# Attention scores and maxima as pairs of 64-row products, in eight long stretches a unit

## The reference, cut to what matters

```
x = layernorm(x)                                       # per token, 256 channels
q, k, v = x @ w_q[h], x @ w_k[h], x @ w_v[h]           # 16 heads of 64
a = softmax(where(query < key, -inf, q @ k.T / 8))     # 1024 x 1024 per head
y = a @ v ;  out = concat_heads(y) @ w_o
```

## Time and profile before

| | |
|---|---|
| median of three runs | 2221.36 us (2218.73 to 2223.20) |
| span of the profiled execution | 2217.0 us |
| PE, PEld, DVE busy | 97%, 72%, 66% of the span |
| ACT, POOL busy | 45%, 62% |
| one regular unit of the attention | 32.39 us |

### The profile page before, as it was taken

One profiled execution on the slowest core, in us unless ns is written; L12 is line 12 of the kernel. 1 busy time (PEld: TensorE's weight loads), 2 busy tenths in 40 slices (PEclk: granted clock), 3 DMA queues, 4 the chain that ended last, 5 costly groups with the idle time before them and its releaser, 6 DMA issues.

```text
span 2217.0 us, 34079 instructions
## 1 busy us (share of the span) xinstructions
PE 2144.5 (97%) x12130; PEld 1600.3 (72%) x12130; DVE 1463.6 (66%) x3344; ACT 1003.0 (45%) x1908; POOL 1375.0 (62%) x1242
## 2 busy tenths in 40 slices
PE   7998999999999999999999999999999999999998
PEld 5446888889876666766667666567666588889997
DVE  7375687676757666476775577874877636975654
ACT  6202543454355554254553354552554425444443
POOL 4313675777457676456674567664677846777774
PEclk9999999999999999999999999999999899999999
DMA  4524553655432212221322131221220244545552
GB/s 133 185 95 122 136 141 97 150 141 134 96 96 58 58 49 57 67 77 49 77 62 70 52 86 48 58 67 58 67 77 24 74 134 115 135 114 146 122 150 40
DMA packets 145048, 206.04 MB, mean 93 GB/s; under 512 B 19432, under 2 KB 112112, under 8 KB 144880
## 3 DMA queue, kind: packets, MB, share of 16 engines
q1 hardware_dynamic: 120304, 170.30, 25.7%
q0 software_dynamic: 24576, 33.57, 9.1%
HBM read 130.03 MB, written 39.85 MB: 77 GB/s over the span
## 4 chain that ended last, share of the span: by engine, by line
PE 74%; DVE 8%; POOL 4%; issue 3%; ACT 2%; DMA 1%; SPq 1%; POOLq 0%; DVEq 0%; ACTq 0%
PE psum L1337 12%; PE psum L1506 11%; PE psum L1358 11%; PE psum L1408 8%; PE psum L1471 7%; PE psum L1487 6%; PE psum L1531 5%; PE psum L1422 4%; PE psum L1436 3%; PE psum L1516 3%; POOL t_acc L2478 2%; DVE f_hhi L2215 2%; DVE f_hlo L2217 1%; PE psum L1449 1%; DVE f_wlo L2190 1%
## 5 line engine op out<-in xcount | busy, mean ns | idle before, releaser
L1782 ACT ACTIVATE t_p<-psum 128x512 f32<-128x512 f32 (+3 forms) x768 | 323.6, 492 | 294.0 <-PE psum L1487 285.7
L2478 POOL TENSOR_TENSOR t_acc<-t_acc,t_p 128x1024 f32<-128x1024 f32 (+3 forms) x256 | 416.9, 1629 | 14.5 <-ACT t_p L1782 0.5
L2397 POOL TENSOR_TENSOR f_wlo<-f_wst,f_whi 128x256 fp32r<-128x256 f32 x256 | 221.8, 943 | 149.0 <-ACT f_whi L1715 148.9
L1506 PE MATMUL psum<-t_p,t_v 128*64 128x512 f32 (+3 forms) x1536 | 289.2, 497 | 5.0 <-POOL t_p L2458 5.0
L1358 PE MATMUL psum<-f_whi,f_hhi 128*128 128x256 f32 x992 | 286.4, 289 | 7.1 <-DVE f_hlo L2217 7.0
L1358 PE MATMUL psum<-f_whi,f_hlo 128*128 128x256 f32 x992 | 280.8, 283 | 0.0
L1358 PE MATMUL psum<-f_wlo,f_hhi 128*128 128x256 f32 x992 | 280.6, 283 | 0.0
L2215 DVE CAST f_hhi<-f_h 128x512 fp32r<-128x512 f32 x256 | 142.2, 556 | 203.5 <-ACT f_h L1733 202.9
L1733 ACT ACTIVATE f_h<-psum 128x512 f32<-128x512 f32 x256 | 153.0, 598 | 271.5 <-PE psum L1337 260.0
L1471 PE MATMUL psum<-t_qa,t_ka 128*128 128x512 f32 (+3 forms) x768 | 224.1, 372 | 1.8 <-DVE t_mx L2263 0.8
L2478 POOL TENSOR_TENSOR t_acc<-t_p 128x768 f32<-128x768 f32 x64 | 134.5, 2102 | 136.9 <-PE psum L1516 133.6
(11 more groups left out here) (297 smaller groups left out, 4452.4 us busy)
## 6 DMA issues: line engine op xcount, KB each, us to landing
f_wst<-in_L_ffn_w SPq DMA_DIRECT2D x64, 1024.0 KB, 5.3
t_ka<-t_ka SPq DMA_DIRECT2D x64, 256.0 KB, 3.5
t_qb<-t_qa SPq DMA_DIRECT2D x64, 256.0 KB, 3.9
t_wk<-wkT SPq DMA_DIRECT2D x32, 256.0 KB, 4.3
t_wq<-wqT SPq DMA_DIRECT2D x32, 256.0 KB, 4.0
t_wv<-wvT SPq DMA_DIRECT2D x16, 512.0 KB, 4.7
normal<-f_xy SPq DMA_DIRECT2D x5, 1024.0 KB, 5.6
a_x<-in_L_attn_a_x SPq DMA_DIRECT2D x4, 1024.0 KB, 8.1
```

What stands on the lines that cost most here:

```text
L1506: m = pe.matmul(k.bank[6][i * DH:(i + 1) * DH, q0:BANK], v[:, kt, vs:vs + DH], p[:, i, q0:BANK], start=(kt == 0), stop=(kt == last), skip_ ...
L1782: act.activation(p[:, i, q0:], k.bank[bank][:, q0:], ACT.Exp, scale=1.0 / float(np.sqrt(k.DH))).then_inc(k.drained[bank], 1)
L2397: m = pool.tensor_tensor(t["wlo"][n % 2][:, i, ks], t["wst"][:, i, ks], t["whi"][n % 2][:, i, ks].bitcast(F32), ALU.subtract)
L2478: pool.tensor_tensor(acc[:, :, q0:], (p0 if kt == 1 else acc)[:, :, q0:], p[:, :, q0:], ALU.add).then_inc(k.p_acc, 1)
```

## The change

The q and k parts are kept as four tiles `khi`, `klo`, `qhi`, `qlo` in which the pair's two heads lie in the two halves of the partitions, as the projection leaves them. Nothing is doubled or moved: `qk_double` and the DMA of `max_rows` are gone. A tile's scores are four products a head, each with 64 rows: high.high, high.low, low.high, and ones against `t_neg`. All are issued as pairs, head 0 in the upper half of the array and head 1 in the lower, into two banks. All maxima parts are such pairs too.

`t_neg` now holds the negated maxima spread over 64-row halves (row n has block n's maxima at block n's columns, zero elsewhere). DVE makes it in one instruction of 72 rows by 1024 columns from the transposed maxima and a tile of minus ones. It is one buffer, and the first scores of a unit wait on PE, ahead of all their products, for it (`wait_drained(("rows", u))`).

A unit is now eight stretches: for g = 0, 1, 2 a row stretch (scores of four key tiles and, after each, the next unit's maximum part) and a column stretch (denominators and weighted values of these tiles); a stretch of full products after the column stretch of g = 0 (`first_work`: projections, values, output) and after that of g = 2 (`last_work`: projection, the transposed maxima, projection, output). There are eight `t_p` buffers.

```diff
-        self.NP = 4
+        self.NP = 8
...
-            kept = [{}, {}]
-            for m in ("ka", "qa", "kb"):
-                for hd in kept:
-                    hd[m] = sb("t_" + m, [P, L], F32R)
-            qb = t["qb"][n] = sb("t_qb", [P, 2, L], F32R)
-            t["heads"][n] = [dict(hd, qb=qb[:, i, :]) for i, hd in enumerate(kept)]
+            t["heads"][n] = {m: sb("t_" + m, [P, L], F32R) for m in ("khi", "klo", "qhi", "qlo")}
...
+        t["minus"], t["mx1"] = sb("t_minus", [P, NBLK]), sb("t_mx1", [P, 2, NBLK - KPC])
...
+        t["neg"] = sb("t_neg", [P, NBLK, P], F32R)
...
-        parts = [(n, c, min(BANK, (n + 1) * P - c * BANK))
-                 for c in range(self.NC) for n in range(self.KPC * c, self.NBLK)]
-        return [p for p in parts if p[2] > BANK // 2], [p for p in parts if p[2] <= BANK // 2]
+        return [[(n, c, (n + 1) * P - c * BANK if diagonal else BANK) for n in range(n0, n0 + self.KPC)]
+                for n0, c, diagonal in ((0, 0, True), (self.KPC, 0, False), (self.KPC, 1, True))]
+
+    def stretch_tiles(self, g):
+
+        return [(min(g, 1), self.KPC * max(g - 1, 0) + i) for i in range(self.KPC)]
 
     def head_rows(self, i):
 
-        return slice(i * self.DH, (i + 1) * self.DH), slice((1 - i) * self.DH, (2 - i) * self.DH)
+        return slice(i * self.DH, (i + 1) * self.DH)
+
+    def qk_place(self, j):
+
+        return (0, 2, 1, 3)[j] + 1
...
+        def project(u, *parts):
+            for j in parts:
                 self.qk_product(u, j)
                 self.qk_low(u, j)
...
+        def normalize(u, c):
+            self.sum_rows(u, c)
+            self.scale_rows(u, c)
+            if u % NHP == NHP - 1:
+                b = u // NHP
+                if b < B - 1:
+                    self.out_load(b, c)
+                extra.append(output(b, c))
+
+        def row_halves(u, g):
+
+            for i, (c, kt) in enumerate(k.stretch_tiles(g)):
                 self.scores(u, c, kt)
...
+                if u + 1 < U:
+                    self.row_max(u + 1, *maxima[g][i])
+                    self.part_max(u + 1, *maxima[g][i])
+                yield
+
+        def column_halves(u, g):
+
+            if g == 0 and u:
+                self.divide(u - 1, 1)
+            for c, kt in k.stretch_tiles(g):
+                self.weigh(u, c, kt)
+                self.add_up(u, c, kt)
+            if g == 1:
+                self.divide(u, 0)
+                normalize(u, 0)
+            elif g == 0 and u:
+                normalize(u - 1, 1)
+
+        def first_work(u):
+
+            yield from project(u + 1, 1, 3)
+            if (u + 2) % NHP == 0 and u + 2 < U:
+                yield from prepare((u + 2) // NHP)
+            for _ in range(value_pieces((u + 1) % NHP)):
+                next(state["values"])
+                yield
+            yield from pieces(2)
+
+        def last_work(u):
+
+            if u + 2 < U:
+                yield from project(u + 2, 0)
+            self.max_rows(u + 1)
+            yield
+            if u + 2 < U:
+                yield from project(u + 2, 2)
+            yield from pieces(3)
...
+            for _ in project(1, 0, 2):
+                pass
+            for u in range(U - 1):
                 if u % NHP == 0:
                     state["rows"] = between(u // NHP)
+                if u + 2 < U:
+                    self.qk_load(u + 2)
+                for g in range(3):
+                    for _ in row_halves(u, g):
+                        pass
+                    column_halves(u, g)
+                    pump(state["rows"])
+                    if g != 1:
+                        for n, _ in enumerate((last_work if g else first_work)(u)):
+                            pump(state["rows"])
+                            if state["scored"] < 2 or n < 2:
+                                pump(state["route"])
+            yield from last_unit(U - 1)
...
+    def row_max(self, u, n, c, w):
+
+        k, pe, heads = self.k, self.e, self.k.t["heads"][u % 2]
+        self.wait_ge(k.a_qk, 2 * k.NC * u + (2 if n < k.KPC else 4))
+        banks = [self.take(("max", u, n, c, i), self.work_bank()) for i in range(2)]
+        for i, bank in enumerate(banks):
+            hd = k.head_rows(i)
+            pe.matmul(k.bank[bank][:, 0:w], heads["qhi"][hd, n * P:(n + 1) * P], heads["khi"][hd, c * BANK:c * BANK + w],
+                      start=True, stop=True).then_inc(k.filled[bank], 1)
...
+        pe.transpose(k.bank[bank][0:k.MROWS, 0:P], t["mx"][:], k.ident[:]).then_inc(k.filled[bank], 1)
...
-    def high_scores(self, u, c, kt):
+    def scores(self, u, c, kt):
 
         k, pe, t = self.k, self.e, self.k.t
         q0, qs, ks = self.score_slices(c, kt)
-        for i in range(2):
-            bank = self.take(("st", u, c, kt, i), self.work_bank())
-            hd = t["heads"][u % 2][i]
-            pe.matmul(k.bank[bank][:, q0:], hd["ka"][:, ks], hd["qa"][:, qs], start=True, stop=False)
-
-    def scores(self, u, c, kt):
-        k, pe, t = self.k, self.e, self.k.t
-        q0, qs, ks = self.score_slices(c, kt)
-        banks = [k.where["st", u, c, kt, i][0] for i in range(2)]
+        heads = t["heads"][u % 2]
         if c == 0 and kt == 0:
-            self.wait_ge(k.t_const_d, 4 if u else 2)
             hp = u % k.NHP
             v = min(4 + 2 * hp, 16) - 1
             self.wait_drained(("v", u // k.NHP, v // 4, v % 4))
-            for h in range(2):
-                self.wait_ge(k.q_dup[u % 2][h][1], DMA * (u // 2 + 1))
-            self.wait_ge(k.q_rows[u % 2], DMA * (u // 2 + 1))
-        for i in range(2):
-            hd = t["heads"][u % 2][i]
-            pe.matmul(k.bank[banks[i]][:, q0:], hd["kb"][0:k.QROWS, ks], hd["qb"][0:k.QROWS, qs], start=False,
-                      stop=True).then_inc(k.filled[banks[i]], 1)
+            for j in range(2 * k.NC):
+                self.wait_drained(("qk", u, j))
+            self.wait_drained(("rows", u))
+        banks = [self.take(("st", u, c, kt, i), self.work_bank()) for i in range(2)]
+        neg = t["neg"][:].rearrange("p n j -> p (n j)")
+        for a, (keys, queries) in enumerate((("khi", "qhi"), ("khi", "qlo"), ("klo", "qhi"))):
+            for i, bank in enumerate(banks):
+                hd = k.head_rows(i)
+                pe.matmul(k.bank[bank][:, q0:], heads[keys][hd, ks], heads[queries][hd, qs], start=(a == 0), stop=False)
+        for i, bank in enumerate(banks):
+            hd = k.head_rows(i)
+            pe.matmul(k.bank[bank][:, q0:], k.ones[hd, :].bitcast(F32R), neg[hd, qs], start=False,
+                      stop=True).then_inc(k.filled[bank], 1)
...
-        for i in range(2):
-            hi, (first, _) = t["heads"][u % 2][i]["qa" if j // k.NC else "ka"], k.head_rows(i)
-            act.copy(hi[first, c * BANK:(c + 1) * BANK],
-                     k.bank[bank][i * k.DH:(i + 1) * k.DH, :]).then_inc(k.a_qk, 1)
+        hi = t["heads"][u % 2]["qhi" if j // k.NC else "khi"]
+        act.copy(hi[:, c * BANK:(c + 1) * BANK], k.bank[bank]).then_inc(k.a_qk, 1)
...
+        dve.memset(t["mx"][:], 0.0).then_inc(k.t_const_d, 1)
+        dve.memset(t["neg"][:].bitcast(F32), 0.0).then_inc(k.t_const_d, 1)
+        dve.scalar_tensor_tensor(out=t["minus"][:], in0=k.ident[:, 0:k.NBLK], scalar=-1.0,
+                                 in1=k.ident[:, k.DH:k.MROWS], op0=ALU.mult, op1=ALU.subtract).then_inc(k.t_const_d, 1)
...
+        self.wait_ge(k.a_qk, 2 * k.NC * u + k.qk_place(j))
+        dve.tensor_tensor(heads["qlo" if is_q else "klo"][:, cs], k.bank[bank],
+                          heads["qhi" if is_q else "khi"][:, cs].bitcast(F32), ALU.subtract).then_inc(k.drained[bank], 1)
...
-        if u > 1:
-            self.wait_ge(k.q_rows[u % 2], DMA * (u // 2))
-        dve.tensor_scalar(t["neg"][u % 2][:], k.bank[bank][0:2 * k.NBLK, 0:P], -1.0, None, ALU.mult).then_inc(k.drained[bank], 1)
+        self.wait_ge(k.t_const_d, 3)
+        if u:
+            self.wait_filled(("st", u - 1, 1, 2 * k.KPC - 1, 1))
+        rows = slice(0, k.MROWS)
+        dve.tensor_tensor(t["neg"][rows], spread(k.bank[bank][rows, 0:P], 1, k.NBLK), spread(t["minus"][rows], 2, P),
+                          ALU.mult).then_inc(k.drained[bank], 1)
...
-    def qk_double(self, u, is_q):
-        k, sp, DH = self.k, self.e, self.k.DH
...
-            src = hd["qa" if is_q else "ka"][first, :]
-            dst = hd["qb"][0:DH, :] if is_q else hd["ka"][other, :]
...
-            sp.dma_start(dst.bitcast(F32), src.bitcast(F32)).then_inc(k.q_dup[u % 2][i][is_q], DMA)
...
-        sp.dma_start(row.bitcast(F32), t["neg"][u % 2][:].bitcast(F32)).then_inc(k.q_rows[u % 2], DMA)```

PE's rows are shown where the kernel before has its mixed order, in a unit with values (`t_p,t_v` is `weigh`, `t_acc,ones` is `divide`, `t_ka,t_qa` with x4 or in the short widths a maximum; order lists a weight pair by its output rows):

```order
L1516 MATMUL psum<-t_acc,ones 64x512 x2
L1506 MATMUL psum<-t_p,t_v 64x256 x2
```

(68 more changed lines are left out.)

315 lines of the change are left out of this document (86 added, 229 removed).

## The result

| | before | after |
|---|---|---|
| time, us (4 runs each; median, range) | 2220.4 (2218.7 to 2223.2) | 2249.3 (2248.1 to 2250.9) |
| span of the profiled execution | 2217.0 | 2246.3 |
| first exponent of the attention at | 627.4 | 633.3 |
| from there to the second expert stage | 1184.0 | 1206.9 |
| a regular unit | 32.39 | 33.32 |

The changed kernel is slower: ratio 1.0127, 95% interval 1.0115 to 1.0140. The forecast was 2223 us with a range of 2180 to 2265, so the range holds the time, but the likeliest case was 26 us too low. The table's first exponent is where ACT turns to it (it loads a table for 1.28 us first).

A forecast was written before the change was run, and what follows sets the result against it. PE's instruction stream was taken to bound the attention. 2217.0 - 70 (saved) + 37 (ring) + 28 + 6 (`t_neg`) = 2218, +2 for small waits and 4.3 between span and median: 2223 us, range 2180 to 2265.

The forecast's parts named there:

- PE's stream: PE's attention instructions: fewer changes of form (1.4 us) and paired short maxima (0.35) save 1.75 us a unit, 56 in all.
- ring of banks: Diagonal row stretches: PE waits for ACT's exponents to free banks, 0.6 us each over 62 stretches, 37 us.
- `t_neg`: Unit hand-over: scores wait 1.1 us for DVE's negated maxima, 25 times, 28 us; plus 6 for routing or normalization steps ahead.
- waits for the maxima's DMA, and the clock: Removed DMA of the maxima: two 2.2 us waits and a 1.7 us clock loss after each go, together 8 us.
- other waits at normalizations and values: Small waits of PE at normalizations, put at +2 us in the sum.
- tail of the attention: End of the attention: the output product's wait for POOL's scaling, with the clock after it, goes: 6 us (0 to 10).
- rival 2: Twenty narrow pairs a unit run at instruction pace, 0.16 us instead of 0.115: 22 us more, 2245 us; chance 0.14.
- The unit of 32.6 us: Among the signs to look for in the trace: a unit of some 32.6 us.
- The middle stretch, put at nothing: Middle row stretch, all tiles 512 wide: PE issues 1.6 us of work before needing the bank, so nothing is lost.
- Rival 3: Each of 25 waits for `t_neg` brings PE's clock down, costing 43 us: 2265 us; chance 0.10.
- Rival 1: Waits mostly hidden, POOL takes over, at most half of 71 us stays: 2186 us, down to 2170; chance 0.27.
- The 0.6 us a unit that I gave POOL: Around the middle row stretch: without the other waits, POOL would hold PE up by some 0.6 us a unit, 19 us.

The follow-up runs named there:

- e1: Changed kernel with the transposed maxima ahead of both projection pieces at a unit's end instead of between them: 2216.8 us, ratio 0.9979 to the kernel before.
- e2: Probe on the changed kernel: first tile of each diagonal row stretch gets half its exponents (256 columns) from the second unit on: 2237.7 us, ratio 1.0065.
- e10: Probe: e6 with exponents of all four tiles of the diagonal row stretches cut to 128 columns: 2197.1 us, ratio 0.9871 to the kernel before.
- e3: Changed kernel with the maxima of the diagonal row stretches in falling widths instead of rising ones: 2265.6 us, ratio 1.0193 to the kernel before.
- e4b: Changed kernel with e1's order and a projection piece moved behind the first tile of both diagonal row stretches: 2209.8 us, ratio 0.9971 to the kernel before.
- e12: The kernel of e4b timed again, beside a repeat of e1 on one chip: 2213.5 us, ratio 0.9953 to the kernel before.
- e5: Probe on the changed kernel: DVE takes the diagonal maxima over 128 columns alone from the second unit on: 2245.5 us, ratio 1.0125.
- e6: Probe on the changed kernel: e1's order, e2's shorter exponents and e5's shorter maxima together: 2201.4 us, ratio 0.9927 to the kernel before.
- e9: Changed kernel with the first unit's 12 maximum pairs one between two expert pieces instead of two: 2247.4 us, ratio 1.0108 to the kernel before.

## Why the prediction was right or wrong

Terms of the sum, in us over the whole kernel:

| term | forecast | measured | from |
|---|---|---|---|
| PE's stream | -56 | -62 | 1.93 x 32, from a regular unit |
| ring of banks | +37 | +51 | 0.83 x 62 |
| `t_neg` | +34 | +32 | the 23 waits; e1 |
| waits for the maxima's DMA, and the clock | -8 | -1 | -4.4, and four falls of the clock for two |
| other waits at normalizations and values | +2 | +5 to 7 | waits for `t_mx`, 4.9, and smaller ones |
| tail of the attention | -6 | -4 | 72.5 to 68.4 us, see below |
| before the first exponent | 0 | +6 | 627.4 to 633.3 |
| sum | +3 | +27 to +29 | span: +29.3 |

**PE's stream.** Right, and a little too cautious. Wide pairs cost 0.23, narrow ones 0.11 and 0.12, as taken from the singles; rival 2 (0.16) is out. The form's changes are there: 0.89 for three pairs after the denominators against 0.68 inside a stretch. The pairs with an increment of a semaphore (line 1458 and the maxima) take 0.23 like those without, as the prediction had read it from the earlier trace rows. So the price of some 26 ns for each increment, which the Trainium skill gives in "TensorE: Matmul & The Clock Gate", section on the per-tile semaphore tail, does not show from start to start here. Two sums of the prediction are off. The unit of 32.6 us does not follow from its own terms: 32.39 - 1.75 + 1.2 + 1.1 is 32.9. And 2218 + 2 + 4.3 is 2224, not 2223.

**The ring of banks: the step that was mis-sized.** The mechanism is right (e2, e10), and so is its first wait: 0.45 was counted for the third tile, and PE starts it at 725.55 instead of 725.09, 0.46 late. What was left out comes after it. The second tile's maximum already waits for the first tile's first exponent (0.19 of the 0.46). The wide maximum at the end needs the bank of tile three's first exponent, and the first pair after each wait takes up to 0.1 more. A diagonal stretch so loses 0.83 us where 0.6 were counted. The middle stretch, put at nothing, is not quite free either: its third tile's first three pairs take 0.80 to 0.83 instead of 0.68 (this is inside the measured stream). And the count followed ACT alone. DVE empties half of a row stretch's banks. It has two transposes and a reciprocal ahead of the maxima in a unit's last diagonal stretch, 1.7 us from 723.25 on, and in e10, where ACT is quick, it holds PE by 0.56 us there. The bound of 0.9 held the price; the value of 0.6 was too low. The Trainium skill, "TensorEngine Tiling (Array Packing)", section PSUM Bottleneck, says that packing does not speed up the emptying of PSUM. e3 and e10 agree (16 us more and 0.56 us a stretch through DVE); the prediction had set it aside because no row showed it.

**`t_neg`.** Right in mechanism, place and size: 14 waits of 1.03 us (a regular unit of e1 is 1.19 shorter), six of 2.0 to 2.8 where a routing or normalization step stood ahead on DVE, three others of 0.3 to 1.7, and none at eight of the 31 hand-overs. e1 takes all but one away. What the forecast left out is the clock behind the six.

**The clock.** Rival 3 had it that 1.1 us a unit would bring the clock down; waits of 1.03 us never did. But of the six long waits four did: behind waits of 2.45, 2.38, 2.45 and 2.75 us PE was granted 0.50 for 3.4 us, from about 1104.6, 1374.2, 1480.0 and 1613.2 us on. Two others, 2.04 and 2.48 us, left it alone. The window after the first, against the earlier trace rows, and then the window around the wait of 2.48 us:

```profile
1104.60:1108.00 3.40, 3.40 (x28) 2.81 (x24) 2.17 (x11) 2.43 (x7) 1.23 (x3) 0.50 0.00 0
1443.00:1449.00 6.00, 4.79 (x44) 3.44 (x46) 5.75 (x18) 2.96 (x8) 2.08 (x6) 1.00 0.01 1
```

So the two falls that came after the removed DMA's waits came back as four: the prediction took the six longer waits as 6 us of time and didn't ask what they do to the clock.

**The tail.** From unit 30's last column stretch to the second expert stage it took 72.5 us before and takes 68.4 now, so the size is near the forecast. The path is mostly another, and that is luck. The wait for POOL's scaled output did fall, from 1.9 to 0.9 us, with no fall of the clock behind it. But PE now waits 5.1 us for POOL's sum and 1.3 for `t_neg`, where before it waited 4.3 for POOL's masks. And the mean granted clock of the tail rises from 0.88 to 0.95: PE stood at half for some 17 us before and for some 7 now. None of this was counted. (The 1.3 us stand in the table's row of `t_neg` too.)

**Rival 1** (waits mostly hidden, POOL next) is out: e10 took most of the waits away, and POOL took nothing back in a regular unit. The 0.6 us a unit that I gave POOL was too dark.

**Before the first exponent.** Nothing was forecast here. 3.4 of the 5.9 us arise at 250 us in expert code that the change does not touch: ACT stands still for 3.6 us, put down to no engine or queue of this core.

```profile
ACT f_h L1711 <- remote: 4.4, 2, 3.6
```

PE waits 2.8 us behind it instead of 1.0, and its clock falls: from 255 to 260 us the mean granted clock is 0.69 where it was 1.00 before. That makes the rest of the 3.4. It is no fixed property of the kernel: the trace of e4b is without this gap, that of e12, the same kernel, has it; so have eight more kernels of the experiments, and e5 and e6 have not. The kernel before was traced once, without it. So 3.4 of the 29.3 us between the two spans come from this; how often it comes in either kernel, and what holds ACT, stays open. Of the rest some 2 us lie between 560 and 629 us, where the first unit's maxima stand among expert pieces; e9 could not settle it.

## What to carry over

When products are packed and become cheaper, count the ring of banks for every engine that empties it, with all that stands ahead of it on that engine, and not for the slowest chain alone: here ACT and DVE came within 0.3 us of each other in a unit's last diagonal stretch (0.83 and 0.56 us of waits), and shortening either one brought little. A small instruction that becomes a 1.2 us one belongs ahead of work that PE can do without it; its place in the order was worth 32 us, and with it the packing brings 0.2%. A piece that is put in as cover takes a bank of the same ring, and helps only if its own emptying is over when the ring comes round.

## Of the hardware

- Row pairs of 64 rows, one in each half, accumulating into two banks, ran side by side: 0.23, 0.17 to 0.18, 0.12 and 0.11 us a pair for 512, 384, 256 and 128 columns, the price of one 128-row product in the earlier trace rows (0.23 to 0.24, 0.12 and 0.11 for 512, 256 and 128).
- PE's waits for a bank that ACT empties show on its weight loads and hide in the modelled end of the product before: 20.0 us there, 1.0 us on PE itself, for a loss of some 51 us by the chain.
- In the changed kernel's attention the clock fell to half after four of six idle stretches of 2.0 to 2.8 us, and after none of fourteen of 1.03 us.
- A change of form costs PE 0.15 us into the column form (2.30 for sixteen instructions after row pairs, 2.15 after other columns) and some 0.21 into row pairs (0.89 for three pairs after denominators, 0.68 inside a stretch).
